# Loading two x tiles first, and giving the first bucket of edges 24 fixed looks with products between them, in a two-layer graph network kernel

## The reference

```
xn   = layernorm(x)                                   # 625 x 1024, no scale or shift
A_r[d, s] = number of edges s -> d of kind r          # 20000 edges sorted by d, 8 kinds
u    = xn @ root + bias + sum_r (A_r xn / count_r) @ weight[r]
k, v = xn @ Wk + bk, xn @ Wv + bv                     # linear attention beside it
```

## Time and profile before

| | |
|---|---|
| median of three runs | 2555.28 us (2554.99 to 2557.93) |
| the profiled execution: its time | 2553.05 us |
| its span | 2551.2 us |
| PE busy over the span | 2369.5 us (93%), 11841 matmuls |
| mean granted clock of TensorE | 0.967 |

### The profile page before, as it was taken

How to read it: one execution, slowest core, us unless ns; L and a number is a source line. 1 busy time by engine, 2 the same in 40 slices (tenths; PEclk the granted TensorE clock), 3 DMA queues, 4 the chain that set the end, 5 groups by cost and what they waited for, 6 DMA issues and landing times.

```text
span 2551.2 us, 30997 instructions
## 1 busy us (share of the span) xinstructions
PE 2369.5 (93%) x11841; PEld 1914.4 (75%) x11841; DVE 1405.1 (55%) x2399; ACT 848.1 (33%) x1052; POOL 267.8 (10%) x243
## 2 busy tenths in 40 slices
PE   6999999999999999999889999986959999898998
PEld 4788887777777777777767777875747779776666
DVE  6786353233333333443689886635864333558976
ACT  3132231111121121121157675632744122133542
POOL 3000320000000000020111111002120110203000
PEclk9899999999999999999889999997979999999999
DMA  4255723433122231323688999766973422253984
GB/s 143 54 137 132 150 88 107 123 99 91 56 69 67 83 91 34 103 86 114 225 278 306 343 353 292 267 199 188 319 264 109 135 74 67 82 164 123 329 279 150
DMA packets 168011, 406.67 MB, mean 159 GB/s; under 512 B 69491, under 2 KB 69780, under 8 KB 167836
## 3 DMA queue, kind: packets, MB, share of 16 engines
q1 hardware_dynamic: 145362, 344.06, 42.1%
q0 software_dynamic: 17008, 47.45, 6.4%
q10 hardware_dynamic: 5466, 12.78, 1.8%
HBM read 360.49 MB, written 56.76 MB: 164 GB/s over the span
## 4 chain that ended last, share of the span: by engine, by line
PE 81%; DVE 8%; DMA 4%; issue 3%; ACT 2%; SPq 1%; DVEq 0%; POOL 0%; ACTq 0%; POOLq 0%
PE PS L308 17%; PE PS L309 16%; PE PS L310 16%; PE PS L1145 7%; PE PS L921 4%; PE PS L563 2%; PE PS L1435 2%; DVE low L300 2%; PE PS L1804 2%; PE PS L1811 2%; PE PS L1813 2%; PE PS L1812 2%; PE PS L3033 2%; PE PS L327 1%; PE PS L2249 1%
## 5 line engine op out<-in xcount | busy, mean ns | idle before, releaser
L300 DVE TENSOR_TENSOR low<-raw,high 128x1024 fp32r<-128x1024 f32 x467 | 568.3, 1256 | 126.3 <-ACT high L288 123.3
L288 ACT ACTIVATE high<-raw 128x1024 fp32r<-128x1024 f32 x476 | 484.1, 1056 | 312.3 <-PE PS L310 246.5
L308 PE MATMUL PS<-high,xt_high 128*125 128x512 f32 x1280 | 518.3, 405 | 29.3 <-DVE xt_low L336 10.5
L309 PE MATMUL PS<-low,xt_high 128*125 128x512 f32 x1280 | 511.7, 400 | 0.0
L310 PE MATMUL PS<-high,xt_low 128*125 128x512 f32 x1280 | 510.0, 398 | 0.0
L308 PEld LDWEIGHTS PS<-high,xt_high 128*125 128x125 f32 x1280 | 241.5, 189 | 93.0 <-DVE xt_low L336 11.8
L310 PEld LDWEIGHTS PS<-high,xt_low 128*125 128x125 f32 x1280 | 240.9, 188 | 62.5
L309 PEld LDWEIGHTS PS<-low,xt_high 128*125 128x125 f32 x1280 | 241.5, 189 | 57.9
L1169 ACT ACTIVATE y_high<-PS 125x512 fp32r<-125x512 f32 x80 | 47.8, 598 | 506.7 <-PE PS L310 506.7
L1180 DVE TENSOR_TENSOR y_low<-PS,y_high 125x512 fp32r<-125x512 f32 x80 | 55.3, 691 | 290.4 <-ACT y_high L1169 290.4
L1145 PE MATMUL PS<-y_high,a_kind 125*125 125x512 f32 x400 | 158.4, 396 | 0.0
(11 more groups left out here) (516 smaller groups left out, 3890.5 us busy)
## 6 DMA issues: line engine op xcount, KB each, us to landing
raw<-in_L_ffn_ew SPq DMA_DIRECT2D x96, 512.0 KB, 5.5
raw<-in_L_gnn_weight SPq DMA_DIRECT2D x64, 512.0 KB, 5.2
raw<-in_L_ffn_k_w SPq DMA_DIRECT2D x64, 512.0 KB, 8.5
raw<-in_L_ffn_q_w SPq DMA_DIRECT2D x64, 512.0 KB, 10.2
raw<-in_L_ffn_v_w SPq DMA_DIRECT2D x64, 512.0 KB, 7.3
raw<-in_L_ffn_f_w SPq DMA_DIRECT2D x64, 512.0 KB, 6.3
adjacency<-a_stage SPq DMA_DIRECT2D x10, 1120.0 KB
a_kind<-adjacency POOLq DMA_DIRECT2D x8, 1367.2 KB, 8.7
```

The source lines that it names most:

```text
L288: a.e.activation(high_of(i)[:, 0:w], RAW[PLACE_OF[i]][:, 0:w], ACT.Copy).then_inc(*a.step(part_high, 1, [("high", i)]))
L300: v.e.tensor_tensor(LOW[p][:, 0:w], RAW[p][:, 0:w], high_of(i)[:, 0:w], ALU.subtract).then_inc(*v.step(signal, 1, [("low", i)]))
L308: p.e.matmul(dst, xh[:, kt, xs], wh[:, c], start=first and j == 0, stop=False)
L309: p.e.matmul(dst, xh[:, kt, xs], wl[:, c], start=False, stop=False)
```

## The change

It has these parts:

1. SP issues x 0, x 1, part 0, part 1, x 2, part 2, x 3, part 3, x 4, then the rest. No low part but 123 to 125 is made by GpSimd; DVE makes parts 0 to 5 too.
2. PE transposes x 0 and x 1, then makes tiles 0 and 1 together, part by part in two banks. Tiles 2 and 3 follow their transposes. DVE normalizes only x 0 and x 1; for x 2 to 4 it computes a shift and ACT applies scale and shift. The order of DVE's and ACT's work follows this.
3. The edge transposes all stand ahead of tile 4, the transposes of the bounds behind it, and tile 5 follows. The part of DVE's arithmetic that only serves the flag `many` comes after `bounds`.
4. Bucket 0 has LOOK0 = 24 fixed looks, and after each four of them PE makes one of the half tiles 12 to 17. What bucket 0 needs beyond 24 still runs in the loop. After bucket b > 0 comes half tile 17 + b, and three half tiles are left behind bucket 39.

```diff
     def low_on_gpsimd(i):
-        return i < 6 or i in (123, 124, 125)
+        return i in (123, 124, 125)
...
+    def halves(c):
+        return c // 2, c % 2
+
+    def half_after(b):
+        return 17 + b
+
+    def first_look(b):
+        return LOOK0 + LOOK * (b - 1) if b else 0
...
         turn(0)
-        fill(0)
         turn(1)
+        p.wait_ge(at("pads"))
+        for j, part in enumerate(Wk[0]):
+            for n in range(2):
+                p.wait_ge(at("xl", "x", n))
+                ins = rows(p, bank(4 + n)[0:PT, :], XTH, XTL, cols(n), part, (2 * j, 2 * j + 1), j == 0, j == 3)
+                if j == 3:
+                    ins.then_inc(*p.mark("fill", n))
         turn(2)
-        fill(1)
         turn(3)
+        fill(2)
         turn(4)
-        fill(2)
+        fill(3)
...
-            fill(3 + h)
+        fill(4)
         p.wait_ge(at("bucket bounds"))
...
-            for k in range(LOOK):
-                n = LOOK * b + k
+            some = LOOK if b else LOOK0
+            for k in range(some):
+                n = first_look(b) + k
                 p.wait_ge(at("one hot", n))
-                look(e, ps, n % 5, k == 0, k == LOOK - 1).then_inc(*p.mark("looked", n))
+                look(e, ps, n % 5, k == 0, k == some - 1).then_inc(*p.mark("looked", n))
+                if b == 0 and k % 4 == 3:
+                    fill_half_tensor(p, *halves(12 + k // 4))
...
-            fill_half_tensor(p, 6 + b // 2, b % 2)
-        for n in range(26, 30):
-            fill_half_tensor(p, n, 0)
-            fill_half_tensor(p, n, 1)
+            if b:
+                fill_half_tensor(p, *halves(half_after(b)))
+        for c in (57, 58, 59):
+            fill_half_tensor(p, *halves(c))
...
+        def normal(t):
+            a.wait_ge(at("x shift", 2 if t < 4 else 4))
+            e.activation(XN[:, t, :], XN[:, t, :], ACT.Identity, bias=lnx[:, 1, t:t + 1], scale=rstd[:, t:t + 1]).then_inc(*a.mark("xn", t))
+
         high_parts(a, 2)
         high(0)
-        high_parts(a, fill_to(0, 1))
         high(1)
+        high_parts(a, 4)
+        normal(2)
+        normal(3)
         high(2)
+        high_parts(a, 5)
+        high(3)
+        normal(4)
+        high_parts(a, 6)
         fill_out_scalar(a, 0)
...
+        def shifts(a, b):
+            deviations(v, a, b)
+            v.wait_ge(v.last)
+            e.scalar_tensor_tensor(lnx[:, 1, a:b], lnmv[:, a:b, 0], -1.0, rstd[:, a:b], op0=ALU.mult, op1=ALU.mult).then_inc(*v.mark("x shift", a))
+
-        stats(0, 1)
-        normal(0, 1)
-        stats(1, 3)
+        stats(0, 2)
+        normal(0, 2)
+        low_parts(v, 2)
         low(0)
-        normal(1, 3)
-        stats(3, 5)
         low(1)
+        stats(2, 3)
+        low_parts(v, 3)
+        stats(3, 4)
+        low_parts(v, 4)
+        shifts(2, 4)
+        stats(4, 5)
         low(2)
-        normal(3, 5)
+        shifts(4, 5)
         fill_out_vector(v, 0)
         low(3)
-        low(4)
-        low_parts(v, fill_to(1, 1))
+        low_parts(v, 5)
         fill_out_vector(v, 1)
...
         for t in range(TT):
             move_rows(s, XN[:, t, :], A["x"][t * PT:(t + 1) * PT, :], xsem[t], "x in", t)
-            if t < TT - 1:
-                load_parts(s, t + 1)
+            if 0 < t < TT - 1:
+                load_parts(s, (0, 2, 3, 4)[t])
         load_parts(s, 11)
-        load_parts(s, 15, at("bounds"))
+        load_parts(s, 15, at("many"))
```

More of the change, by code:

```diff
@@ L621, in start_scalar @@
         e.activation(E2[:, :, 1], bank(3)[:, 0:164], ACT.Copy).then_inc(*a.mark("edges"))
+        high_parts(a, fill_to(4, 1))
+        fill_out_scalar(a, 3)
         high_parts(a, fill_to(5, 1))
@@ L627, in edges_scalar @@
         fill_out_scalar(a, 5)
+        for c in range(6):
+            high_parts(a, fill_to(*halves(12 + c)))
+            if c in (3, 5):
+                fill_out_scalar(a, 5 + c // 2)
         for b in range(NB):
@@ L634, in edges_scalar @@
             e.activation(stg[:, :, :, 16 * j:16 * j + 16], ps[0:PT + 1, 0:640].rearrange("p (m d r) -> p m r d", m=TT, d=16), ACT.Copy).then_inc(*a.mark("copied", b))
[L635 to L641, removed]
+            if b % 2:
+                fill_out_scalar(a, half_after(b - 1) // 2)
+            if b:
+                high_parts(a, fill_to(*halves(half_after(b))))
+        high_parts(a, fill_to(*halves(58)))
+        fill_out_scalar(a, 28)
+        high_parts(a, fill_to(*halves(59)))
         fill_out_scalar(a, 29)
@@ L704, in start_vector @@
             e.tensor_scalar(hi, hi, most, None, op0=ALU.mult).then_inc(*v.mark("edge hi", h))
-            fill_out_vector(v, 2 + h)
-            low_parts(v, fill_to(3 + h, 1))
-        low_parts(v, fill_to(5, 1))
+            if h == 0:
+                low(4)
+                fill_out_vector(v, 2)
+            else:
+                low_parts(v, fill_to(3, 1))
+                fill_out_vector(v, 3)
         v.wait_ge(at("edge bounds", 1))
@@ L731, in edge_columns @@
         v.wait_ge(at("edges"))
-        some = slice(0, LOOK)
+        n, dst = (LOOK, EC[:, b % 2, :, :]) if b else (LOOK0, EC0[:, :, :])
+        some = slice(0, n)
         if not points.counting:
-            some = bass.ds(v.e.snap(v.register(f"bound{b % 4}"), min_val=0, max_val=164 - LOOK), LOOK)
-        v.e.tensor_copy(EC[:, b % 2, :, :], E2[:, some, :]).then_inc(*v.mark("columns", b))
+            some = bass.ds(v.e.snap(v.register(f"bound{b % 4}"), min_val=0, max_val=164 - n), n)
+        v.e.tensor_copy(dst, E2[:, some, :]).then_inc(*v.mark("columns", b))
     def edges_vector(v):
@@ L746, in edges_vector @@
             v.wait_ge(at("columns", b))
-            for k in range(LOOK):
-                n = LOOK * b + k
+            for k in range(LOOK if b else LOOK0):
+                n = first_look(b) + k
+                col = EC[:, b % 2, k, :] if b else EC0[:, k, :]
                 if n > 4:
                     v.wait_ge(at("looked", n - 5))
-                one_hot(e, n % 5, b, EC[:, b % 2, k, 0:1], EC[:, b % 2, k, 1:2]).then_inc(*v.mark("one hot", n))
+                one_hot(e, n % 5, b, col[:, 0:1], col[:, 1:2]).then_inc(*v.mark("one hot", n))
+                if b == 0 and k % 4 == 3:
+                    if k // 4 in (3, 5):
+                        fill_out_vector(v, 5 + k // 8)
+                    low_parts(v, fill_to(*halves(12 + k // 4)))
             if not points.counting:
@@ L829, in start_gpsimd @@
         e.iota(bsti[:, :], [[128, NB]], base=0, channel_multiplier=0).then_inc(*g.mark())
+        for i, (most, least) in enumerate(((164 - LOOK, 164 - LOOK0), (LOOK, LOOK0))):
+            g.wait_ge(g.last)
+            e.memset(looks[:, i, :], float(most)).then_inc(*g.mark())
+            g.wait_ge(g.last)
+            e.memset(looks[:, i, 0:1], float(least)).then_inc(*g.mark(*("looks",) if i else ()))
         mixer_gpsimd(g, M0)
```

47 lines of the change are left out of this document (24 added, 23 removed).

## The result

The changed kernel takes 2541.14 us (median of 10 runs, 2535.97 to 2551.32) against 2555.14 for the kernel before. The ratio is 0.9951, with a 95% interval of 0.9937 to 0.9964: 12.5 us faster (the two medians differ by 14.0), and surely faster, by 9 to 16 us. The forecast was 2538, a gain of 17.9.

A forecast was written before the change was run, and what follows sets the result against it. PE was taken as the bound from 115 to 272 us, with gains only ahead of that: 21.3 us won less 3.4 for low clock, 17.9 us, giving 2538 us; range 2531 to 2546.

The forecast's parts named there:

- A: The whole change gains as summed: 12 to 23 us won, 2532 to 2543; chance 0.72.
- B: Smaller gain, 5.2 to 12 us: normalizing slow by DMA (3.9), x 1 late (2.6), low clock (3.4 more); chance 0.12.
- C: No measurable change (within 5.1 us): bucket 39's adjacency lands late, or DVE feeds bucket 0 no sooner; chance 0.06.
- D: Slower: bucket 0's mix of looks and half tiles runs long at the lower clock; 5 us slower, 2560; chance 0.04.
- Start: Kernel start: x 1 at 8.2 us, first product at 17.5 us instead of 19.04.
- The choice of 0.77 us for normalizing: Start: each x tile normalizes in 0.77 us with GpSimd out of the way; if DMA slows it, 3.9 us later.
- Tile 2: PE stands 4.0 us ahead of tile 2 for DVE's read of tile 0, at 36.7 us.
- one low stretch for each of the two stands: After PE's stands of 4.0 and 2.3 us the clock falls, one stretch each, 3.4 us lost together.
- Bounds and first look: Edge and bounds work beside tiles 2 to 5: PE stands 2.3 us, first look at 63.3 us instead of 72.52.
- if it is later: Edge transposes ending up to 4 us after 49.6: tile 4 still covers it, but transposes ahead of tile 4 would wait.
- Bucket 0: Looks mixed with half tiles take 25.8 us; bucket 0 closes at 89.1 us.
- the same buckets and half tiles at the same pace: Rest of the stage behind bucket 0: PE-bound at the same pace, no extra cost.

The follow-up runs named there:

- shift_first: Changed kernel with DVE's chain for x 4 and its read of tile 0 ahead of the low part of x 2; ratio 0.9903, repeated 0.9933.
- short_adds: Changed kernel with GpSimd adding only 8 of 512 columns of each key tile, so k is wrong elsewhere; ratio 0.9922.
- looks_ready: shift_first with low parts 8 and 9 and the read of tile 5 behind bucket 0's first four one-hot pairs; ratio 0.9914.
- bucket_alone: Kernel before with only part 4 of the change (flag `many` computed behind the bounds), the start as before; ratio 0.9961.
- gpsimd_low: Changed kernel with low parts 0 to 5 made by GpSimd again, as before the change; ratio 0.9971.

## Why the prediction was right, and where its sum was off

**How right.** The gain of 12.5 us lies just inside A (12 to 23), and its interval, 9 to 16 us, reaches into B (5.2 to 12). The measured time fits both, and excludes C (within 5.1 us) and D. That A holds rests on the marks of one execution, which show where the missing 5.5 us are; that they added up to no more is in part luck.

**Start.** First product at 18.19 us, 0.7 later than summed, for a later x 1. The choice of 0.77 us for normalizing held: 1.53 for two, at full DMA traffic. The Trainium skill, "SBUF — State Buffer", section "SBUF: two separate sides", says that VectorE and GpSimd share a port pair as an exclusive lock and that traffic doesn't slow an engine; the rows agree, with 0.16 us against 2.28 for line 354 beside a GpSimd subtraction.

**Tile 2.** The wait was forecast at 4.0 us and measured at 4.3, at the named place.

**The clock.** I counted one low stretch for each of the two stands, 3.4 us lost. The first stand brought 6.8 us at the lower level. Its first 1.6 us fell into the stand itself, so PE lost 2.6 us there (tile 2 took 8.1 us instead of 5.56). The second was forecast at 2.3 us and was 1.24; 3.4 us at the lower level followed from about 70 us on, some 1.6 lost. Such a level is no sure price of that wait: of the eight other executions with the same 1.24 us, five had one there and three (shift_first twice and short_adds) had none. Together 4.2 instead of 3.4.

**Bounds and first look.** Forecast 63.3, measured 67.18. Of these 3.9 us, 0.7 are the start, 2.6 the clock of tile 2 (which the sum carried elsewhere), 0.96 the wait ahead of the edge transposes and 0.7 short gaps around the transposes; 1.1 go off, since PE stood 1.24 us and not 2.3. The reason for that stand was wrong too. I had put low parts 8 and 9 and 1.56 us for reading registers in front of the first pair; but DVE was through with the low parts at 65.0 and went on without such a gap, and then it idled 0.30 us for the end of tile 5, which it reads ahead of the first pair. In looks_ready, with no low parts there, the gap of 1.49 us is back. The wait of 0.96 us is the step that I put aside with "if it is later": behind it stand DVE operations of 1.41 and 1.32 us that last so long for GpSimd's additions.

**Bucket 0.** Its 25.8 us were right where it was measured alone (25.7). In the changed kernel it took 28.3: 1.0 for the stall of the one-hot key, and 1.6 for the low clock level. In shift_first, with the stall and at full clock, it took 26.7.

**The rest.** The term most off is the one that I priced at nothing: "the same buckets and half tiles at the same pace". It cost 2.4 us (2.5 in bucket_alone): 1.25 in bucket 4, 0.5 in bucket 1, 0.3 in bucket 6. The balance for the changed kernel: start 0.7, edge wait and gaps less the shorter stand 0.6, looks 1.0, clock 4.2 - 3.4 = 0.8, rest 2.4, together 5.5; and 17.9 - 5.5 = 12.4, what the stage's end shows.

**The end of the stage.** No wait for the adjacency was forecast (rival C), and PE shows none; up to 330 us it waits once, 0.73 us for a low part at 318.30, where it waited 0.98 before. The rows of DVE and ACT:

```profile
289.49 1.32 DVE L836 CAST sel_tmp<-sel_int 128x2 f32<-128x2 int32 x1 [4.50 <-DMA sel_int<-in_L_ffn_index]
...
292.90 0.79 ACT L1026 ACTIVATE q_cols_L_mix<-PS,bias_q_L_mix 128x628 f32<-128x628 f32 x1 [7.02 <-DVE x_twice L1119]
```

Line 1026 (968 before) did come 1.5 us later into the products of `Wq`, 8.8 instead of 7.2 behind their start. By the rows it came behind DVE's chain for the chosen rows, which stood 4.50 us for its own load (2.59 before); with two banks of lead PE didn't notice.

**The rivals.** D was not seen: 0.96 in bucket 0. Nor was C: the first look came 5.3 us sooner than before. Of B's list, slow normalizing didn't happen, x 1 was 0.8 us late and not 2.6, and more low clock was partly there; its range is not ruled out by the total.

## What to carry to other kernels

When work is moved between engines, look at what stands beside it and not only at how long it takes: beside an addition of 1.30 us on GpSimd, DVE's line 760 took 1.12 us in the changed kernel, and 0.19 in short_adds. When a filler is moved forward in a schedule, its helpers move too; check the engine with the least to spare in the places where they land, and the loads that they wait for. And an engine that stands before its next input is a place for work that comes right behind: two lines moved there took 2.8 us off the wait and some 2.6 off the low clock behind it, where the whole change had brought 12.4 (the stage's end itself came 8 to 9 us sooner, in part by chance).

## What was not expected of the hardware

The slow DVE operations beside GpSimd were not the large ones alone: steps on 125 x 2 numbers took 2.28 and 2.25 us (gpsimd_low), and one-hot keys, casts and copies 1.1 to 1.4, while statistics of 1.23 to 1.29 us for two halves kept their time (gpsimd_low, at 24.51 us, within GpSimd's subtractions of 22.95 to 27.88). And the clock at the start differs between executions that do the same: the first product took 0.76 us in some and 0.47 in others.
